# Stages of the last batch placed in the last iteration, with two buffers for x2

## The chip, the cores and the metric

The kernel runs on one core of a Trainium2 chip. The metric is the device time of one execution in microseconds (us). In the profile PE is TensorE (matrix multiply, PEld its weight loads), DVE is VectorE, ACT is ScalarE, POOL is GpSimd, SP is SyncE, which here issues every DMA.

## The reference, cut to what matters

```python
def reference(x, W_attn, W_proj, W, b, V_r, C):      # x: (4, 2048, 256)
    x = x + 0.5 * ffn(layernorm(x))                  # ffn(z) = z @ W.T + b + (z @ V_r) @ C.T
    x = x + attn(layernorm(x))
    x = x + 0.5 * ffn(layernorm(x))
    return x

# attn: 16 heads of width 16, causal; scores s = q.k / 4
# weight of a pair = polymax(s) = (s*s + 1 if s > 0 else 1 - s/100) / 1000   (no softmax sum)
# y = weights @ v; result y @ W_proj
```

## The kernel before

The 4 x 2048 rows are cut into 16 chunks of 512 rows (`NCH`), four to a batch (`CPB`). Each chunk goes through three stages. A (tables `A_*`): layer norm, z1T, ffn, giving x1. B (`B_*`): layer norm, q, k, v and the state sums. C (`C_*`): when the chunk's y is complete for all 16 heads, `proj` (y @ W_proj plus x1, into `x2`), layer norm `ln3` into `z3`, transposes `z3T`, `out` (the second ffn added to `x2`), and the store.

Attention runs as 16 iterations (`ITERS`): one for each batch and each group of four heads. An iteration has 40 tiles, so 80 half tiles: one in each slot of a hand-written plan (`order()`). In a slot TensorE does a half tile's scores, in each second slot the values matmuls of the tile three tiles back (`LAG`), and then the pieces of stage jobs that the plan places there. The scores lie in two PSUM buffers; DVE and ACT raise them into `rp`, POOL and ACT square them, TensorE sums them into y. Window c of an iteration is query chunk c; its y is complete, and copied by ACT (L806), at slots 13, 29, 53 and 83 (83 is slot 3 of the next iteration, or of what follows the last).

A stage table says at which slots after its start a job begins on TensorE: `C_SHORT` has proj at 0 and 4, ln3 from 8, z3T at 20 and 21, out at 22 and 26; `C_FULL` has 24 and 28, 32, 65 and 67, 71 and 75. A proj or out job has four pieces (slots) of 8 matmuls; two jobs make 64 matmuls. DVE empties a proj or out job one slot before the end of its four plus one (L889, L894), ACT empties z3T (L780). ln3 steps: DVE's statistics in steps 0 to 3, aggregation in step 4, scales in step 7 (L869 to L871), ACT's square root in step 8, POOL's normalisation in steps 8 to 11 (L686), the bias in steps 12 to 15 (L694). Each engine runs its instructions in the order of the slots.

SP's queue is ordered by slots too. `load_c` (L534, L535) loads `y_c` and `x1c` for a chunk, 12 slots ahead of proj at most. It waits until the chunk's y has been stored (`store_y`, L541) and until proj of the chunk before is emptied (there is one `y_c` and one `x1c`). The finished x2 is stored at L624; the first DVE write of the next chunk's proj waits for that store (`out_stored`), as there is one `x2`.

The plan before: C of chunk n-4 in iteration n from 4 to 14 (`C_FULL`). In iteration 15: chunk 11 at slot 0, chunk 12 at 27, chunk 13 at 54, all `C_SHORT`. After the last iteration (`drain`): five slots, then chunk 14 whole at slot 85 and chunk 15 whole at slot 117, counted from the start of iteration 15. What follows at `o.again` runs only if scores below -100 can occur; here it doesn't.

Of the kernel before, what the change touches and what calls it, by code (L numbers as in the profile page):

```python
# [12 lines left out]
P = 128  # L13
# [98 lines left out]
B_EARLY = {"qT": (0, 2), "k": (4, 8), "v": (22, 26), "kT": (30, 32), "state": (31, 33, 34, 35)}  # L112
C_SHORT = {"proj": (0, 4), "ln3": 8, "z3T": (20, 21), "out": (22, 26)}
# [80 lines left out]
def order():  # L194
# [10 lines left out]
    for n in range(1, ITERS):  # L205
        at = o.stretch(NHALF, range(NHALF))
        if n + CPB < NCH:
            o.stage(n + CPB, at, B_FULL)
        if n + CPB + 1 < NCH:
            o.stage(n + CPB + 1, at, A_FULL)  # L210
        if CPB <= n < ITERS - 1:
            o.stage(n - CPB, at, C_FULL)
    o.stage(NCH - 5, at, C_SHORT)
    o.stage(NCH - 4, at + 27, C_SHORT)
    o.stage(NCH - 3, at + 54, C_SHORT)
    assert o.next_half == ITERS * NHALF
    o.drain = o.n
    o.stretch(LAG + 2)
    o.stage(NCH - 2, o.stretch(32), C_SHORT)
    o.stage(NCH - 1, o.stretch(40), C_SHORT)  # L220
# [52 lines left out]
def build(nc, x_in, w_attn, w_proj, ffn_w, ffn_b, ffn_v, ffn_c, out):  # L273
    ctx = ExitStack()
    with ctx:
# [53 lines left out]
        x2 = sb("x2", [P, NB, DM])  # L329
# [147 lines left out]
        def _(sp):  # L477
# [73 lines left out]
            for x in o.jobs:  # L551
                if (x.kind, x.i) == ("ffn", 1):
                    put(x.empty_at + 1, "x1", x.chunk)
                if (x.kind, x.i) == ("qT", 1):
                    put(x.empty_at + 1, "qT", x.chunk)
                if (x.kind, x.i) == ("v", 1):
                    put(x.empty_at + 1, "v", x.chunk)
                if (x.kind, x.i) == ("state", NB - 1):
                    put(x.empty_at + 3, "state", x.chunk)
                if (x.kind, x.i) == ("kT", KC - 1):  # L560
                    put(x.empty_at + (2 if x.chunk < EARLY else 8), "parts", x.chunk)
                    if x.chunk < CPB:
                        put(x.empty_at + 5, "kq", 0, x.chunk)
                if (x.kind, x.i) == ("proj", 0):
                    put(max(x.start - 12, o.again if x.chunk >= NCH else 0), "c", x.chunk)
                if (x.kind, x.i) == ("out", 1):
                    put(x.empty_at + 1, "out", x.chunk)
            for n in range(ITERS):
                for c in range(CPB):
                    put(o.copy_slot[n * CPB + c] + 1, "y", n, c)  # L570
# [4 lines left out]
            def slot(s):  # L575
                for what, *args in at.get(s, ()):
# [43 lines left out]
                    if what == "out":  # L620
# [3 lines left out]
                        sp.dma_start(out_d[CH * c:CH * c + CH, :].rearrange("(i p) d -> p i d", p=P), x2[:]).then_inc(out_stored, 16)  # L624
# [22 lines left out]
        def _(pool):  # L647
# [30 lines left out]
            def normalise(k, src, dst, chunk, i):  # L678
                if i == 0:
# [4 lines left out]
                    if k == "ln2":  # L684
                        pool.wait_ge(job_done, o.made("z1T", chunk, 1))
                ins = pool.tensor_scalar(dst[:, i, :], src[:, i, :], rstd[k][:, i:i + 1], shift[k][:, i:i + 1],  # L686
# [17 lines left out]
            def slot(s):  # L704
# [20 lines left out]
                for k, chunk, step in o.steps.get(s, ()):  # L725
                    src, dst = {"ln1": (x_sb, z), "ln2": (x1, z), "ln3": (x2, z3)}[k]
# [129 lines left out]
        def _(dve):  # L856
# [10 lines left out]
            def scales(k, chunk):  # L867
                dve.wait_ge(sd_done[k], chunk + 1)
                nc.vector.reciprocal(rstd[k][:], sd[k][:]).then_inc(rstd_done[k], 1)  # L869
# [3 lines left out]
            def empty(x):  # L873
# [10 lines left out]
                if kind == "proj":  # L884
                    if i == 0:
                        dve.wait_ge(c_loaded, (a + 1) * 32)
                        if a > 0:
                            dve.wait_ge(out_stored, a * 16)
                    nc.vector.scalar_tensor_tensor(x2[:, 2 * i:2 * i + 2, :], two, 1.0 / DIVISOR, x1c[:, 2 * i:2 * i + 2, :],  # L889
                                                   ALU.mult, ALU.add).then_inc(done, 1)  # L890
                if kind == "out":
                    if i == 0:
                        dve.wait_ge(x2b_ready, a + 1)
                    nc.vector.tensor_tensor(x2[:, 2 * i:2 * i + 2, :], two, x2[:, 2 * i:2 * i + 2, :], ALU.add).then_inc(done, 1)  # L894
# [5 lines left out]
            def slot(s):  # L900
# [28 lines left out]
                for k, chunk, step in o.steps.get(s, ()):  # L929
                    x = {"ln1": x_sb, "ln2": x1, "ln3": x2}[k]  # L930
# [227 lines left out]
```

## Time and profile before

| | us |
|---|---|
| median of three runs | 1956.75 |
| lowest, highest | 1953.23, 1956.96 |
| the profiled execution, its own time | 1957.39 |
| its span, first to last instruction | 1955.6 |
| TensorE busy | 1667.1 (85%) |
| DVE, ACT, POOL busy | 1328.0, 1363.4, 1323.8 |
| mean granted TensorE clock | 0.964 |

Busy time is the sum of an engine's instructions. A stretch is read by cutting the span at a recurring instruction; here at ACT's copies of y (L806), of which there are 64, four to an iteration. "Idle before, releaser" tells how long an engine stood still before an instruction and which instruction ended that.

### The profile page before, as it was taken

How to read it: one execution, taken by the hardware profiler on the slowest of the kernel's cores; microseconds unless marked ns; L12 is line 12 of the kernel's file. 1: busy time of each engine (PE TensorE's matmuls, PEld its weight loads, DVE VectorE, ACT ScalarE, POOL GpSimd, SP SyncE). 2: the span in 40 equal slices, each digit the busy share in tenths (PEclk: the TensorE clock that was granted, in tenths of full speed). 3: DMA queues.
4: the chain of work that ended last, by engine and by line, in shares of the span. 5: the costliest groups of instructions: out<-in, count | busy, mean ns of one | idle time of the engine just before them, and what ended most of it. 6: DMA issues, size and time to landing. Idle time of an engine off the chain costs nothing.

```text
span 1955.6 us, 66923 instructions
## 1 busy us (share of the span) xinstructions
PE 1667.1 (85%) x27158; PEld 807.2 (41%) x27158; DVE 1328.0 (68%) x3313; ACT 1363.4 (70%) x2178; POOL 1323.8 (68%) x1419
## 2 busy tenths in 40 slices
PE   4687889898989899898989989898988889898884
PEld 2344334343434444353444435343444444434332
DVE  1465677776767777677777767777677777777652
ACT  1244568787878777777778778776877888886650
POOL 3354558787878767778776768877677767676552
PEclk9898889999999999999999999999999999999996
DMA  2343433332315242343424333341513231413111
GB/s 74 122 135 120 128 102 93 93 104 79 112 50 152 67 118 76 113 117 90 121 59 129 92 101 102 95 133 32 159 50 118 70 95 49 117 39 106 37 36 58
DMA packets 155190, 183.14 MB, mean 94 GB/s; under 512 B 22012, under 2 KB 129660, under 8 KB 152836
## 3 DMA queue, kind: packets, MB, share of 16 engines
q1 hardware_dynamic: 154884, 178.82, 31.3%
q8 instruction: 221, 3.62, 0.8%
q14 instruction: 85, 0.70, 0.1%
HBM read 102.43 MB, written 76.30 MB: 91 GB/s over the span
## 4 chain that ended last, share of the span: by engine, by line
PE 52%; ACT 17%; DVE 15%; issue 8%; POOL 4%; DMA 3%; SPq 0%; ACTq 0%; DVEq 0%; POOLq 0%
PE y_ps L977 19%; PE score L977 16%; PE bank L977 13%; DVE rp L912 9%; ACT rp L820 7%; ACT rp L836 4%; PE bank L1003 3%; ACT rp L840 3%; POOL z L686 2%; DVE lin L918 1%; DMA part_scratch<-parts 1%; ACT lin L826 1%; DVE qk_max L924 1%; DMA out_dram<-x 1%; DVE bnst_ln L937 1%
## 5 line engine op out<-in xcount | busy, mean ns | idle before, releaser
L912 DVE TENSOR_SCALAR rp<-score 128x512 f32<-128x512 f32 (+2 forms) x1728 | 944.2, 574 | 223.4 <-PE score L977 219.7
L977 PE MATMUL score<-qs,ks 96*32 96x512 bf16 (+3 forms) x10240 | 742.8, 354 | 169.5 <-DVE rp L912 86.1
L724 POOL TENSOR_TENSOR rp<-rp 128x1024 f32<-128x1024 f32 (+1 forms) x416 | 755.7, 1828 | 148.5 <-DVE rp L912 137.2
L820 ACT ACTIVATE rp<-score 128x512 f32<-128x512 f32 (+1 forms) x832 | 458.5, 592 | 292.3 <-PE score L977 289.8
L977 PE MATMUL y_ps<-rp,vt 128*16 128x512 f32 (+3 forms) x5120 | 598.6, 539 | 22.1 <-ACT rp L840 14.2
L977 PEld LDWEIGHTS score<-qs,ks 96*32 96x32 bf16 x10240 | 291.6, 96 | 599.0 <-DVE rp L912 314.1
L836 ACT ACTIVATE rp<-rp,rise 128x1024 f32<-128x1024 f32 (+1 forms) x416 | 464.1, 1145 | 1.4 <-POOL rp L699 1.4
L699 POOL TENSOR_SCALAR_AFFINE_SELECT rp<-rp 128x256 f32<-128x256 f32 (+1 forms) x384 | 184.1, 481 | 312.6 <-ACT rp L820 158.4
L840 ACT ACTIVATE rp<-rp 128x1024 f32<-128x1024 f32 (+2 forms) x224 | 291.1, 1305 | 121.3 <-POOL rp L699 67.6
L918 DVE SCALAR_TENSOR_TENSOR lin<-score,slope_mask 128x128 f32<-128x128 f32 x768 | 215.1, 280 | 0.0
L977 PEld LDWEIGHTS y_ps<-rp,vt 128*16 128x16 f32 x5120 | 133.6, 97 | 102.4 <-ACT rp L840 25.5
L977 PE MATMUL bank<-w_ffn,zT 128*32 128x256 f32 x2048 | 164.1, 411 | 7.4 <-ACT zT L780 7.4
L977 PE MATMUL bank<-w_qkv,z2T 128*32 128x256 f32 x2048 | 150.9, 386 | 9.7 <-ACT parts L797 9.7
L1003 PE MATMUL bank<-ident,z 128*128 128x128 f32 x384 | 70.5, 320 | 50.4 <-POOL z L686 48.1
L686 POOL TENSOR_SCALAR z<-x,rstd_ln,shift_ln 128x256 f32<-128x256 f32 x128 | 72.1, 569 | 59.6 <-DVE shift_ln L871 58.4
L977 PEld LDWEIGHTS bank<-w_ffn,zT 128*32 128x32 f32 x2048 | 70.5, 118 | 84.8 <-issue 54.9
L977 PE MATMUL y_ps<-lin,vt 128*16 128x128 f32 x2048 | 104.4, 273 | 0.0
L977 PEld LDWEIGHTS y_ps<-lin,vt 128*16 128x16 f32 x2048 | 60.4, 96 | 79.7 <-issue 67.4
L977 PEld LDWEIGHTS bank<-w_qkv,z2T 128*32 128x32 f32 x2048 | 65.9, 111 | 61.2 <-issue 27.5
L869 DVE RECIPROCAL rstd_ln<-sd_ln 128x4 f32<-128x4 f32 x48 | 8.5, 177 | 117.5 <-ACT sd_ln L849 117.5
L1003 PEld LDWEIGHTS bank<-ident,z 128*128 128x128 f32 x384 | 48.2, 160 | 89.6 <-issue 78.0
L686 POOL TENSOR_SCALAR z<-x_sb,rstd_ln,shift_ln 128x256 f32<-128x256 f32 x64 | 35.0, 556 | 69.2 <-DVE shift_ln L871 69.2
(78 smaller groups left out, 1392.9 us busy)
## 6 DMA issues: line engine op xcount, KB each, us to landing
part_scratch<-parts SPq DMA_DIRECT2D x16, 1536.0 KB, 7.5
qs<-part_scratch SPq DMA_DIRECT2D x384, 64.0 KB
ks<-part_scratch SPq DMA_DIRECT2D x384, 64.0 KB, 2.4
state_scratch<-st_new SPq DMA_DIRECT2D x16, 528.0 KB
st<-state_scratch SPq DMA_DIRECT2D x64, 132.0 KB
x_sb<-in_L_attn_x_dram SPq DMA_DIRECT2D x16, 512.0 KB, 4.3
x_scratch<-x SPq DMA_DIRECT2D x16, 512.0 KB, 5.3
qT_scratch<-qkT SPq DMA_DIRECT2D x16, 512.0 KB, 3.9
```

The costliest lines, as they stand in the source:

```text
L686: ins = pool.tensor_scalar(dst[:, i, :], src[:, i, :], rstd[k][:, i:i + 1], shift[k][:, i:i + 1], ALU.mult, ALU.add)
L699: pool.affine_select(out=block, in_=block, compare_op=ALU.is_ge, fill=fill, base=0, pattern=[[0, heads_in_it], [1, P]], channel_multiplier ...
L724: pool.tensor_tensor(half, half, half, ALU.mult).then_inc(squared["pool"], 1)
L820: nc.scalar.activation(rp[T % RP_BUFS][:, 2 + v, off:CH], score[H % S_BUFS][:, v, off:CH], ACT.Relu).then_inc(raised["act"], 1)
L826: nc.scalar.activation(lin[D % L_BUFS][:, 2 + v, :], score[H % S_BUFS][:, v, off:off + P], ACT.Copy, scale=SLOPE, bias=ONE).then_inc(lin_d ...
L836: nc.scalar.activation(part, part, ACT.Square, bias=rise[:]).then_inc(squared["act"], 1)
L840: nc.scalar.activation(whole, whole, ACT.Square).then_inc(squared["act"], 1)
L912: nc.vector.tensor_scalar(rp[T % RP_BUFS][:, 2 * u + v, off:CH], score[H % S_BUFS][:, v, off:CH], 0.0, RISE, ALU.max, ALU.add).then_inc(ra ...
L918: nc.vector.scalar_tensor_tensor(lin[D % L_BUFS][:, 2 * u + v, :], score[H % S_BUFS][:, v, off:off + P], ONE / SLOPE, slope_mask[:, 0, :], ...
L924: nc.vector.tensor_reduce(qk_max[:, x.chunk, j:j + 1], qkT[:, j, :], AX.X, ALU.max, apply_absolute_value=True).then_inc(bounded, 1)
L977: return nc.tensor.matmul(*args, start=start, stop=stop, skip_group_check=True)
L1003: ins = nc.tensor.transpose(dst[:, P * blk:P * blk + P], src[:, blk, P * i:P * i + P], ident[:])
```

## The change

`x2` gets two buffers, used by turns of chunks. So the first DVE write of proj(a) waits for a-1 stores and not for a. The plan of stage C changes from iteration 12 on. Iteration 12 holds chunks 8 and 9 (new table `C_HALF`, 40 slots each), 13 and 14 hold chunks 10 and 11 (`C_FULL`). Iteration 15 holds chunk 12 at slot 20 and chunk 13 at slot 50 (`C_SHORT`), and chunk 14 at slot 60 (`C_LATE`, the same figures as `C_SHORT`): its proj is at slots 60 and 64, its z3T at 80 and 81, its out at 82 and 86. Chunk 15 starts at slot 92. A load of C is now issued no earlier than the slot after the chunk's y is copied, and the store of y goes to the head of its slot on SP. Two guards are added: POOL's normalisation ln3 waits until z3T of the chunk before is done, and DVE's scales wait until POOL has used those of the chunk before. By the slots of the plan the load of chunk 12 stands in slot 14, that of 13 in slot 38, that of 14 in slot 54 and that of 15 in slot 84.

```diff
@@ -110,6 +110,8 @@
 A_FIRST = {"z1T": (12, 13), "ffn": (14, 18), "z2T": (34, 35), "ln1": 0, "ln2": 22}
 A_EARLY = {"z1T": (12, 13), "ffn": (14, 18), "z2T": (38, 39), "ln1": 0, "ln2": 22}
 B_EARLY = {"qT": (0, 2), "k": (4, 8), "v": (22, 26), "kT": (30, 32), "state": (31, 33, 34, 35)}
+C_HALF = {"proj": (0, 6), "ln3": 10, "z3T": (24, 26), "out": (28, 34)}
+C_LATE = {"proj": (0, 4), "ln3": 8, "z3T": (20, 21), "out": (22, 26)}
 C_SHORT = {"proj": (0, 4), "ln3": 8, "z3T": (20, 21), "out": (22, 26)}
 
 AGGR, SCALES, ROOT, NORM, BIAS = NB, NB + 3, NB + 4, NB + 4, 2 * NB + 4
@@ -208,16 +210,22 @@
             o.stage(n + CPB, at, B_FULL)
         if n + CPB + 1 < NCH:
             o.stage(n + CPB + 1, at, A_FULL)
-        if CPB <= n < ITERS - 1:
+
+
+        if CPB <= n < ITERS - CPB:
             o.stage(n - CPB, at, C_FULL)
-    o.stage(NCH - 5, at, C_SHORT)
-    o.stage(NCH - 4, at + 27, C_SHORT)
-    o.stage(NCH - 3, at + 54, C_SHORT)
+        if n == ITERS - CPB:
+            o.stage(n - CPB, at, C_HALF)
+            o.stage(n - CPB + 1, at + NHALF // 2, C_HALF)
+        if ITERS - CPB < n < ITERS - 1:
+            o.stage(n - CPB + 1, at, C_FULL)
+    for c, s in ((NCH - 4, 20), (NCH - 3, 50)):
+        o.stage(c, at + s, C_SHORT)
     assert o.next_half == ITERS * NHALF
     o.drain = o.n
-    o.stretch(LAG + 2)
-    o.stage(NCH - 2, o.stretch(32), C_SHORT)
-    o.stage(NCH - 1, o.stretch(40), C_SHORT)
+    o.stage(NCH - 2, at + 60, C_LATE)
+    o.stretch(LAG + 9)
+    o.stage(NCH - 1, o.stretch(32), C_SHORT)
     o.again = o.n
     for c in range(NCH, 2 * NCH):
         o.stage(c, o.stretch(40), C_SHORT)
@@ -326,7 +334,7 @@
         y_sb = [sb(f"y_sb{i}", [P, CH]) for i in range(2)]
         y_c = sb("y_c", [P, KC, CH])
         x1c = sb("x1c", [P, NB, DM])
-        x2 = sb("x2", [P, NB, DM])
+        x2 = [sb(f"x2_{i}", [P, NB, DM]) for i in range(2)]
         z3 = sb("z3", [P, NB, DM])
         z3T = zT
 
@@ -562,12 +570,13 @@
                     if x.chunk < CPB:
                         put(x.empty_at + 5, "kq", 0, x.chunk)
                 if (x.kind, x.i) == ("proj", 0):
-                    put(max(x.start - 12, o.again if x.chunk >= NCH else 0), "c", x.chunk)
+                    last_y = o.copy_slot[(x.chunk // CPB * QUADS + QUADS - 1) * CPB + x.chunk % CPB] if x.chunk < NCH else o.again
+                    put(max(x.start - 12, last_y + 1), "c", x.chunk)
                 if (x.kind, x.i) == ("out", 1):
                     put(x.empty_at + 1, "out", x.chunk)
             for n in range(ITERS):
                 for c in range(CPB):
-                    put(o.copy_slot[n * CPB + c] + 1, "y", n, c)
+                    at.setdefault(o.copy_slot[n * CPB + c] + 1, []).insert(0, ("y", n, c))
                     if n + 1 < ITERS:
                         put(o.half_slot[2 * (n * NT + LAST[c]) + 1] + 2, "q", n + 1, c)
                         put(o.values_slot[n * NT + KEY_LAST[c]] + 1, "k", n + 1, c)
@@ -621,7 +630,7 @@
                         seq, = args
                         c = seq % NCH
                         wait_emptied(sp, "out", seq, 1)
-                        sp.dma_start(out_d[CH * c:CH * c + CH, :].rearrange("(i p) d -> p i d", p=P), x2[:]).then_inc(out_stored, 16)
+                        sp.dma_start(out_d[CH * c:CH * c + CH, :].rearrange("(i p) d -> p i d", p=P), x2[seq % 2][:]).then_inc(out_stored, 16)
 
             for s in range(o.again):
                 slot(s)
@@ -683,6 +692,8 @@
                         pool.wait_ge(job_done, o.made("z2T", chunk - 1, 1))
                     if k == "ln2":
                         pool.wait_ge(job_done, o.made("z1T", chunk, 1))
+                    if k == "ln3" and chunk > 0:
+                        pool.wait_ge(job_done, o.made("z3T", chunk - 1, 1))
                 ins = pool.tensor_scalar(dst[:, i, :], src[:, i, :], rstd[k][:, i:i + 1], shift[k][:, i:i + 1],
                                          ALU.mult, ALU.add)
                 if i == NB - 1:
@@ -723,7 +734,7 @@
                         half = buf[:, 0:2, off:CH]
                         pool.tensor_tensor(half, half, half, ALU.mult).then_inc(squared["pool"], 1)
                 for k, chunk, step in o.steps.get(s, ()):
-                    src, dst = {"ln1": (x_sb, z), "ln2": (x1, z), "ln3": (x2, z3)}[k]
+                    src, dst = {"ln1": (x_sb, z), "ln2": (x1, z), "ln3": (x2[chunk % 2], z3)}[k]
                     if 0 <= step - NORM < NB:
                         normalise(k, src, dst, chunk, step - NORM)
                     if 0 <= step - BIAS < NB and k != "ln2":
@@ -866,6 +877,9 @@
 
             def scales(k, chunk):
                 dve.wait_ge(sd_done[k], chunk + 1)
+                if chunk > 0:
+
+                    dve.wait_ge(z_ready[k], chunk)
                 nc.vector.reciprocal(rstd[k][:], sd[k][:]).then_inc(rstd_done[k], 1)
                 dve.wait_ge(rstd_done[k], chunk + 1)
                 nc.vector.scalar_tensor_tensor(shift[k][:], mv[k][:, :, 0], -1.0, rstd[k][:], ALU.mult, ALU.mult).then_inc(norm_ready[k], 1)
@@ -884,14 +898,14 @@
                 if kind == "proj":
                     if i == 0:
                         dve.wait_ge(c_loaded, (a + 1) * 32)
-                        if a > 0:
-                            dve.wait_ge(out_stored, a * 16)
-                    nc.vector.scalar_tensor_tensor(x2[:, 2 * i:2 * i + 2, :], two, 1.0 / DIVISOR, x1c[:, 2 * i:2 * i + 2, :],
+                        if a > 1:
+                            dve.wait_ge(out_stored, (a - 1) * 16)
+                    nc.vector.scalar_tensor_tensor(x2[a % 2][:, 2 * i:2 * i + 2, :], two, 1.0 / DIVISOR, x1c[:, 2 * i:2 * i + 2, :],
                                                    ALU.mult, ALU.add).then_inc(done, 1)
                 if kind == "out":
                     if i == 0:
                         dve.wait_ge(x2b_ready, a + 1)
-                    nc.vector.tensor_tensor(x2[:, 2 * i:2 * i + 2, :], two, x2[:, 2 * i:2 * i + 2, :], ALU.add).then_inc(done, 1)
+                    nc.vector.tensor_tensor(x2[a % 2][:, 2 * i:2 * i + 2, :], two, x2[a % 2][:, 2 * i:2 * i + 2, :], ALU.add).then_inc(done, 1)
                 if kind == "state":
                     if a * NB + i >= 2:
                         dve.wait_ge(st_added, a * NB + i - 1)
@@ -927,7 +941,7 @@
                     if b < EARLY:
                         split(dve, b, i, step)
                 for k, chunk, step in o.steps.get(s, ()):
-                    x = {"ln1": x_sb, "ln2": x1, "ln3": x2}[k]
+                    x = {"ln1": x_sb, "ln2": x1, "ln3": x2[chunk % 2]}[k]
                     if step == 0:
                         if k == "ln1":
                             dve.wait_ge(x_loaded, (chunk + 1) * 16)
```

## Rows read from the trace of the kernel before

**Rows 1.** The page, part 1: busy time and share of each engine.

```profile
PE 1667.1 (85%) x27158; PEld 807.2 (41%) x27158; DVE 1328.0 (68%) x3313; ACT 1363.4 (70%) x2178; POOL 1323.8 (68%) x1419
```

**Rows 2.** Windows cut at last copies: span, length, PE, PEld, DVE, ACT, POOL, PEclk.

```profile
508.37:611.54 103.17, 92.07 (x1564) 44.07 (x1560) 75.50 (x191) 83.58 (x135) 79.83 (x83) 1.00 0.32 94
611.54:724.12 112.58, 101.09 (x1700) 49.40 (x1696) 80.58 (x204) 85.09 (x138) 84.45 (x91) 0.98 0.34 101
...
1505.75:1598.04 92.29, 81.93 (x1356) 38.02 (x1352) 69.64 (x171) 75.11 (x117) 65.88 (x67) 1.00 0.28 76
...
1690.93:1784.03 93.10, 84.27 (x1396) 39.20 (x1392) 69.43 (x169) 75.11 (x117) 65.94 (x67) 0.98 0.32 87
1784.03:1905.18 121.15, 99.44 (x1492) 44.51 (x1484) 76.95 (x184) 74.02 (x113) 71.80 (x75) 0.94 0.16 47
1905.18:1955.60 50.42, 24.23 (x290) 14.20 (x282) 11.66 (x36) 3.39 (x7) 9.87 (x16) 0.70 0.18 56
```

**Rows 3.** Chain's shares, then waits (total, times, longest us), in iteration 15.

```profile
by line: DVE rp L912 18.7%; PE y_ps L977 15.5%; PE bank L977 12.4%; PE score L977 10.8%; issue 9.1%; DMA out_dram<-x 5.0%; ACT rp L820 4.0%; ACT rp L840 3.2%; POOL rp L724 3.1%; PE bank L1003 2.7%; POOL z L686 2.7%; DVE bnst_ln L937 2.3%; D
...
DVE x L889 <- DMA out_dram<-x: 5.1, 2, 3.2
```

**Rows 4.** Timeline, ACT: copy of the first y of iteration 13 and of iteration 15.

```profile
1606.85 0.63 ACT L806 ACTIVATE y_sb<-y_ps 128x512 f32<-128x512 f32 x1
...
1794.84 0.63 ACT L806 ACTIVATE y_sb<-y_ps 128x512 f32<-128x512 f32 x1
```

**Rows 5.** DMA issues with median us to landing; timeline of two loads.

```profile
y_c<-y_scratch SPq DMA_DIRECT2D x16, 512.0 KB, 5.3
x1c<-x_scratch SPq DMA_DIRECT2D x16, 512.0 KB, 5.8
...
DMA to landing us min/median/max: 5.0/5.8/8.0
...
1799.64 0.40 SPq L534 DMA_DIRECT2D y_c<-y_scratch  x1
1800.09 0.47 SPq L535 DMA_DIRECT2D x1c<-x_scratch  x1
...
1875.77 0.69 DVE L889 SCALAR_TENSOR_TENSOR x<-bank,x1c 128x512 f32<-128x512 f32 x1 [3.15 <-PE bank L977]
1876.55 0.40 SPq L534 DMA_DIRECT2D y_c<-y_scratch  x1
```

**Rows 6.** Timeline, TensorE in iteration 13, slots 20 and 57 to 60.

```profile
1612.32 0.41 PE L977 MATMUL y_ps<-lin,vt 128*16 128x128 f32 x8
...
1655.52 0.83 PE L977 MATMUL score<-qs,ks 96*32 96x512 bf16 x12 [0.20 <-ACT lin L826]
...
1658.61 1.05 PE L977 MATMUL y_ps<-rp,vt 128*16 128x512 f32 x8 [0.23 <-POOL rp L724]
1659.46 0.41 PE L977 MATMUL y_ps<-lin,vt 128*16 128x128 f32 x8
```

**Rows 7.** Timeline, TensorE in iteration 15, z3T of chunk 11 and behind it.

```profile
1805.07 0.63 PE L1003 MATMUL bank<-ident,z 128*128 128x128 f32 x4 [1.60 <-POOL z L686]
...
1807.26 1.92 PE L977 MATMUL y_ps<-rp,vt 128*16 128x512 f32 x8
```

**Rows 8.** Timeline of the tail, after the last y.

```profile
1905.18 0.60 ACT L806 ACTIVATE y_sb<-y_ps 128x512 f32<-128x512 f32 x1 [0.94 <-PE y_ps L977]
...
1912.71 0.40 SPq L534 DMA_DIRECT2D y_c<-y_scratch  x1
...
1917.74 1.94 PE L1003 MATMUL bank<-ident,z 128*128 128x128 f32 x8 [8.31 <-POOL z L686]
...
1920.46 6.29 PE L977 MATMUL bank<-w_ffn,zT 128*32 128x256 f32 x64 [0.78 <-ACT zT L780]
...
1926.57 3.64 PE L977 MATMUL bank<-w_out,y_c 128*32 128x256 f32 x64
...
1932.47 1.29 DVE L889 SCALAR_TENSOR_TENSOR x<-bank,x1c 128x512 f32<-128x512 f32 x2 [4.96 <-DMA out_dram<-x]
```

## The prediction

> **What bounds the kernel now.** I read the page first [rows 1]: TensorE is busy 85% of the span, and the other engines about 70%. Then I cut the span at the copies of the last y of each iteration (slot 3 of the next one) and read each stretch [rows 2]. An iteration with stages A and B beside its attention takes 103.17 us, one with A, B and C 112.58, so one more C costs 9.41 us where TensorE is already full. An iteration with C alone takes 92.29 to 93.10 us, so attention alone takes some 83.2. The last iteration holds three C stages and takes 121.15 us: two more C at 9.4 would make 111.5, so some 10 us are lost to waits there. After the copy of the last y stand 50.4 us in which no engine is full: a serial tail. The change works on these two stretches and loads iteration 12 for it.
>
> Which wait ends last in the last iteration: DVE's proj emptying waits for the store of the chunk before, since both use x2. That is 5.1 us of DVE idleness, and this store holds 5.0% of the stretch on the chain of waits, 6.0 us [rows 3]. The rest are waits at z3T, whose normalisation on POOL stands just ahead of it [rows 7].
>
> **The edits, step by step.** Slots are those of the plan; I count them from the start of the iteration.
>
> **1. Iteration 12 gets C of chunk 9.** One C is 64 proj matmuls, 8 transposes, 64 out matmuls, plus two loads, one store, and the work of DVE, ACT and POOL. Its price as a whole is 9.4 us [rows 2]. C_HALF puts 14 slots between the end of proj and z3T, with 3 slots between POOL's last normalise step and z3T (C_SHORT has 1), so I add only 0.5 us. Sum +9.9. Bounds: 8.3 (bare TensorE work at full speed: 3.64 for 64 matmuls, twice, and half of the 1.94 us of 8 transposes at half speed [rows 8]) and 14.1 (each of the two further C in iteration 15: (121.15 - 92.9)/2). Chunks 10 and 11 only move up one chunk in iterations 13 and 14, at the place where 9 and 10 stood: nothing. Chunk 11's first proj pieces leave the end of stretch 14: -0.5.
>
> **2. The last iteration has less C.** Before, it holds C of 11, 12, 13 up to the last y, but for the last out piece, some 24.4 us of TensorE work. After, it holds 12, 13, proj and z3T of 14 and one piece of out, 8.3 x 2 + 3.6 + 1.0 + 0.5 = 21.7. The difference, 2.7 us, at the rate 9.4/8.3, is -3.1 us.
>
> **3. Two x2.** proj(a) waits for the store of a-2 instead of a-1. That takes away the 6.0 us on the chain. Nothing takes this wait's place, as the store of two chunks earlier issues many slots before. -6.0; bounds -5.1 (the idleness of DVE alone) and -7.7 (a slow stretch of the clock gone with it, 1.7 us, step 6).
>
> **4. A new wait at proj of chunk 12.** It moves from slot 27 to 20; its y is copied at slot 13 and its load is issued at 14 on SP. In iteration 15 the copy starts at 1794.84 and y_c is issued at 1799.64, 4.80 later: the four stores of y and their landing lie between. x1c goes 0.45 behind and needs 5.8 [rows 4, 5]. It lands at copy + 11.05. When does TensorE reach proj? In iteration 13, which has no work beside attention there, the copy of chunk 0 starts at 1606.85, and the last matmuls of slot 20 start at 1612.32 and are issued by 1612.54: copy + 5.7 [rows 4, 6]. So TensorE stands 11.05 - 5.7 = 5.3 us. Behind that instruction are queued all scores, on which DVE and ACT live (two score buffers), so that nothing hides it. I take 4.9 (the landing between its least, 5.0, and its median); bounds 0 (other engines catch up) and 5.5.
>
> **5. A new wait at proj of chunk 14.** proj 14 stands at slot 60; the single y_c is free when proj 13 is emptied at slot 57. The rows of chunk 13 before give this: DVE's second proj starts at 1875.77 just as the matmuls are done, and y_c is issued at 1876.55, 0.8 later [rows 5]. With 0.45 and 5.8 the load lands some 7.1 us after proj 13. From slot 57 to the job of slot 60 iteration 13 takes from about 1655.95 (a third into the score row) to 1659.68, 3.7 us [rows 6]. TensorE stands 3.4 us; bounds 0 and 4.1. SP blocks behind this wait, but its next entry is only the store of chunk 13.
>
> **6. The clock.** After a wait of 1.60 us of TensorE for z, eight y matmuls take 1.92 us instead of 1.05 [rows 6, 7]: half speed, 1.2 instead of 2.4 GHz. The stretch of iteration 15 has a granted clock of 0.94 against 0.98 to 1.00 before [rows 2]. Each new wait should bring one such stretch; two of them at 1.0 us (bounds 0 and 1.7): +2.0.
>
> The Trainium skill, "TensorE: Matmul & The Clock Gate", section "HAM oscillation — how this bites in real kernels", tells that a matmul burst shorter than the load behind it meets a cold array each time, and pays again at each wait. It speaks against putting proj so near to its load. By it both waits cost the whole slow stretch; a sum that left the clock out would be 2.0 lower here and another 3.2 lower in the tail. The trace agrees: 1.92 against 1.05 us.
>
> **7. The guards of z3 and of rstd.** POOL waits for z3T of the chunk before, and DVE's scales for POOL's z: 15 and 45 waits. For all but chunk 14 they are met tens of slots earlier. For 14, DVE reaches the scales at slot 75, POOL's normalise of 13 ends at 69. I take 0; bounds 0 and +3 (POOL six slots late). DVE stands there anyway for ACT's square root.
>
> **8. The tail.** Before, the copy of the last y ends at 1905.78 and the span 49.8 us later. In between stand the whole of chunk 14, then chunk 15: its proj starts at 1926.57, though its y_c was issued at 1912.71 already, and DVE then waits 4.96 us for the store of 14; from the end of its proj emptying, 1932.47 + 1.29 = 1933.76, to the end it is 21.84 us [rows 8]. After, only out of 14 is left (3.6 us) and the load sets the start: stores of y and landing 4.6 (between the 4.2 of chunk 12 and the 6.9 of the last), x1c 0.45 + 5.3: TensorE starts proj 15 at copy end + 10.3. It has been idle for about 7 us then. Before, 8.31 us idle led to 64 out matmuls in 6.29 us instead of the 3.64 of proj, half speed; so proj takes 6.8 us (64 matmuls at the 0.106 us of that fill), and DVE's last emptying 0.9 more: + 18.0. With 21.84 it is 39.8 instead of 49.8: -10.0. Bounds: -13.2 (proj at full speed) and -8 (stores as slow as in the last row, 6.9).
>
> **Sum**: 9.9 - 0.5 - 3.1 - 6.0 + 4.9 + 3.4 + 2.0 + 0 - 10.0 = +0.6 us. On the profiled execution's 1957.39 that is 1958.0; the median of the runs is 1956.75, so the forecast for a median is **1957.4 us**: no change. What the tail gives, the extra C in iteration 12 and the two load waits take back.
>
> **Rivals.** First, **the waits cost little** (faster). TensorE is idle for some 10 us of each light iteration [rows 2]; if these gaps close behind the waits, since DVE, ACT and POOL have caught up, steps 4, 5 and 6 fall from 10.3 to about 2: 1949. For it: POOL and ACT run slots late in the last iteration. Against it: the two score buffers tie DVE to TensorE at each half, and a lost 5 us is lost to both. Second, **a C in a crowded iteration costs 14 us** (slower). This is z3T reached before POOL's z, as in the last iteration, where each further C costs 14.1 instead of 9.4. If C_HALF in iteration 12 and proj 13 and 14 side by side do that, it is +4.7 for one and about as much for the two together: 1957.4 + 7 = 1964. It decides from the point where TensorE reaches z3T before POOL's last normalise step, as it did by 1.60 us for chunk 11 [rows 7]. Third, **the plan does less than it says**: z3T of 14 delays the last y, or the load comes late (x1c took 8.0 us once [rows 5]), so that proj 15 starts at copy + 14. Then the tail gives 6 instead of 10: 1961, just at the border. Fourth, **the tail gives all**, proj 15 at full speed and a quick load: -13.2, 1954.
>
> **How the numbers follow.** Forecast 0.42, with its own range 1953.5 to 1961.3. Waits cheap 0.26 (all faster). Crowded 0.17 (slower). Late load 0.08 (half slower). Full tail 0.07 (a third faster, two thirds within). A change below 0.2%, 3.9 us, can't be told from none. Of the forecast's own chance a tenth falls out on either side, 0.04 each. Faster: 0.26 + 0.02 + 0.04 = 0.32. Slower: 0.17 + 0.04 + 0.04 = 0.25. Within: 0.43. The range from 1947 to 1966 leaves out the outer parts of the first two rivals.
>
> **What would show it.** Step 1: iteration 12 at 102 us instead of 92.3. Steps 2 to 6: the last iteration at 121 to 122, with two waits of TensorE for x1c or y_c of 3 to 5 us ahead of w_out matmuls, and no wait of DVE's proj line for the store. Step 7: no wait of DVE's reciprocal for POOL. Step 8: 39.8 us from the last copy's end to the span's end, with the first proj matmul 10.3 us behind the copy. It is wrong if the last iteration falls under 115 us (first rival) or iteration 12 comes to 106 (second).

## The result and the profile after

The changed kernel takes 1947.5 us (median of four runs, 1944.8 to 1948.7) against 1956.9 before: ratio 0.9950, 95% interval 0.9936 to 0.9965. Measured once more beside its variants it was 1944.3 against 1954.6, ratio 0.9953 (0.9940 to 0.9967). So it is 0.5% faster, by 9.4 and 10.3 us, where no change was forecast. The profiled execution took 1944.84 us, with a span of 1943.1.

The page after, part 1, and the windows cut at the last copies, as in [rows 1] and [rows 2] (length, PE, PEld, DVE, ACT, POOL, granted clock; iterations 12, 13, 14, 15 and the tail):

```profile
PE 1663.6 (86%) x27158; PEld 808.4 (42%) x27158; DVE 1327.9 (68%) x3313; ACT 1364.3 (70%) x2178; POOL 1326.4 (68%) x1419
```

```profile
1499.96:1601.70 101.74, 90.71 (x1480) 43.34 (x1472) 76.87 (x190) 76.89 (x119) 71.10 (x75) 0.97 0.28 74
1601.70:1695.39 93.69, 83.47 (x1360) 38.21 (x1356) 69.61 (x171) 75.16 (x116) 66.04 (x67) 0.98 0.29 75
1695.39:1787.37 91.98, 82.00 (x1366) 37.89 (x1361) 69.65 (x171) 75.18 (x117) 65.98 (x67) 1.00 0.29 77
1787.37:1905.02 117.65, 97.09 (x1464) 44.94 (x1453) 74.99 (x179) 74.33 (x113) 71.94 (x75) 0.93 0.16 48
1905.02:1943.10 38.08, 17.50 (x202) 9.97 (x202) 7.49 (x22) 1.99 (x5) 4.94 (x8) 0.74 0.21 61
```

Where the 12.5 us between the two spans went:

| stretch | before | after | difference | forecast |
|---|---|---|---|---|
| up to the end of iteration 0 | 300.67 | 294.43 | -6.2 | 0 |
| iterations 1 to 11 | 1205.08 | 1205.53 | +0.5 | 0 |
| iteration 12 | 92.29 | 101.74 | +9.5 | +9.9 |
| iterations 13 and 14 | 185.99 | 185.67 | -0.3 | -0.5 |
| iteration 15 | 121.15 | 117.65 | -3.5 | +1.2 |
| tail | 50.42 | 38.08 | -12.3 | -10.0 |

The first row is not the change's. The same stretch of both kernels, before and then after:

```profile
0.00:300.67 300.67, 221.40 (x3144) 113.07 (x3148) 166.85 (x419) 130.77 (x226) 134.28 (x177) 0.88 0.37 114
```

```profile
0.00:294.43 294.43, 215.28 (x3144) 112.31 (x3148) 166.91 (x419) 130.76 (x225) 134.63 (x177) 0.91 0.38 117
```

The work is the same, 3144 matmul records, but TensorE was granted 0.91 instead of 0.88 and was busy 6.1 us less. In the runs below this stretch ends between 294.9 and 301.1 us, with either plan. It scatters, so the experiments are read from the last iterations and the tail, and the medians beside them. These windows scatter too: each is read from one profiled execution, and two such executions of the changed kernel (this one and a0 below) differ by 1.4 us in the last iteration, 1.1 in the tail and 3.0 in iterations 13 and 14. A difference of that size between two runs is not shown by their windows alone.

The two waits that were forecast, in the timeline of the changed kernel (start, us, engine, line, idle before and releaser). First chunk 12, whose y was copied at 1796.18:

```profile
1799.81 0.40 SPq L542 DMA_DIRECT2D y_c<-y_scratch  x1
1800.26 0.85 SPq L543 DMA_DIRECT2D x1c<-x_scratch  x1
...
1801.66 0.41 PE L991 MATMUL y_ps<-lin,vt 128*16 128x128 f32 x8
1805.49 1.08 PE L991 MATMUL bank<-w_out,y_c 128*32 128x256 f32 x8 [3.41 <-DMA x1c<-x_scratch]
1806.32 1.11 PE L991 MATMUL score<-qs,ks 96*32 96x512 bf16 x8
...
1836.44 0.63 PE L1017 MATMUL bank<-ident,z 128*128 128x128 f32 x4 [2.78 <-POOL z L697]
...
1867.92 0.64 PE L991 MATMUL bank<-w_out,y_c 128*32 128x256 f32 x8 [1.99 <-DMA x1c<-x_scratch]
...
1902.19 0.63 PE L1017 MATMUL bank<-ident,z 128*128 128x128 f32 x4 [1.89 <-POOL z L697]
```

The fifth line is chunk 12's scores behind the wait at half speed (1.11 us for eight; 0.64 in e7 below). The sixth is chunk 12's transposes, which wait 2.78 us for POOL's normalised z. The seventh is chunk 14's proj, the last its transposes, which wait for POOL just ahead of the last y's values. The tail, which answers to [rows 8]:

```profile
1905.02 0.60 ACT L817 ACTIVATE y_sb<-y_ps 128x512 f32<-128x512 f32 x1
1905.17 3.66 PE L991 MATMUL bank<-w_ffn,zT 128*32 128x256 f32 x64 [0.22 <-ACT zT L791]
1905.64 1.73 SPq L549 DMA_DIRECT2D y_scratch<-y_sb  x4
...
1908.63 0.40 SPq L542 DMA_DIRECT2D y_c<-y_scratch  x1
...
1914.98 5.99 PE L991 MATMUL bank<-w_out,y_c 128*32 128x256 f32 x64 [6.15 <-DMA x1c<-x_scratch]
...
1921.03 0.69 DVE L903 SCALAR_TENSOR_TENSOR x<-bank,x1c 128x512 f32<-128x512 f32 x1 [1.67 <-PE bank L991]
...
1926.85 1.94 PE L1017 MATMUL bank<-ident,z 128*128 128x128 f32 x8 [5.88 <-POOL z L697]
...
1929.57 5.53 PE L991 MATMUL bank<-w_ffn,zT 128*32 128x256 f32 x64 [0.78 <-ACT zT L791]
```

### The profile page after: what moved, and what is told of

It reads as the page before. It is cut to its first block, busy times and chain, and to the rows that moved or that the text cites. A ratio compares the mean times of both kernels' runs of the same rounds, so it can differ in the third digit from the quotient of the medians.

```text
span 1943.1 us, 66983 instructions
## 1 busy us (share of the span) xinstructions
PE 1663.6 (86%) x27158; PEld 808.4 (42%) x27158; DVE 1327.9 (68%) x3313; ACT 1364.3 (70%) x2178; POOL 1326.4 (68%) x1419
## 3 DMA queue, kind: packets, MB, share of 16 engines
q8 instruction: 222, 3.64, 0.8%
## 4 chain that ended last, share of the span: by engine, by line
PE 54%; ACT 16%; DVE 15%; issue 8%; POOL 4%; DMA 3%; SPq 1%; ACTq 0%; DVEq 0%; POOLq 0%
PE y_ps L991 20%; PE score L991 17%; PE bank L991 14%; DVE rp L926 9%; ACT rp L831 6%; ACT rp L847 4%; PE bank L1017 3%; ACT rp L851 3%; POOL z L697 2%; DVE lin L932 1%; DMA x1c<-x_scratch 1%; ACT lin L837 1%; DMA part_scratch<-parts 1%; DVE qk_max L938 1%; DVE rest L463 1%
## 5 line engine op out<-in xcount | busy, mean ns | idle before, releaser
L991 PE MATMUL bank<-w_ffn,zT 128*32 128x256 f32 x2048 | 159.5, 400 | 5.4 <-ACT zT L791 5.4
L991 PE MATMUL bank<-w_out,y_c 128*32 128x256 f32 x1024 | 81.9, 397 | 12.1 <-DMA x1c<-x_scratch 12.1
```

Of the source, the lines that this page charges most:

```text
L991: return nc.tensor.matmul(*args, start=start, stop=stop, skip_group_check=True)
```

## The experiments

In all of them "last iteration" is the stretch from the copy of the last y of iteration 14 to that of iteration 15, and "tail" runs from there to the end of the span. The slots of chunks 12 and 14 stand as (20, 60) for the changed kernel. Ratios are to the kernel before, run beside the variant. `...` marks what is left out of an edit.

### The parts of the change

**e1: order of SP's queue and guards alone, on the kernel before.**

```diff
-                    put(o.copy_slot[n * CPB + c] + 1, "y", n, c)
+                    at.setdefault(o.copy_slot[n * CPB + c] + 1, []).insert(0, ("y", n, c))
...
+                    if k == "ln3" and chunk > 0:
+                        pool.wait_ge(job_done, o.made("z3T", chunk - 1, 1))
...
+                if chunk > 0:
+                    dve.wait_ge(z_ready[k], chunk)
```

> The kernel before with two small parts of the change alone: the stores of y at the head of their slot on SP, and the two guards (z3 on POOL, rstd on DVE). Theory: neither is on the path; time as before, 1956.9 within 2 us, and the 6 us by which the changed kernel's profile reached the end of iteration 0 earlier (294.4 against 300.7) are scatter of the start. Rival: the order of SP's queue shortens iteration 0; then its last copy comes at 294 to 295 here too and the time is 1951.

Measured: 1957.6 against 1954.1, ratio 1.0024 (1.0004 to 1.0043). Iteration 0 ends at 297.8, the last iteration takes 127.9 us, 6.7 more than before, all of it between the copies of chunks 1 and 2. Both theories missed this. The timeline shows it:

```profile
1818.31 2.74 SPq L541 DMA_DIRECT2D y_scratch<-y_sb  x4
1821.09 0.42 SPq L624 DMA_DIRECT2D out_dram<-x  x1
1824.22 0.69 DVE L893 SCALAR_TENSOR_TENSOR x<-bank,x1c 128x512 f32<-128x512 f32 x1 [7.57 <-DMA out_dram<-x]
```

Both the store of y and the store of chunk 11's x2 stand in slot 30. With y first, x2's store waits behind ACT's copy and four issues, and DVE, which waits for it with one x2, stands 7.57 us instead of 3.2 [rows 3]. In the changed kernel, with two x2, no such wait is left; the order with two x2 wasn't tested by itself. The guards were not tested without the order; no wait for them stands out in the waits of the last iterations.

**e2: two buffers for x2 alone.** A store semaphore for each buffer, the plan as before.

```diff
-        x2 = sb("x2", [P, NB, DM])
+        x2 = [sb(f"x2_{i}", [P, NB, DM]) for i in range(2)]
-        out_stored = sem("out_stored")
+        out_stored = [sem(f"out_stored{i}") for i in range(2)]
...
-                        if a > 0:
-                            dve.wait_ge(out_stored, a * 16)
+                        if a > 1:
+                            dve.wait_ge(out_stored[a % 2], a // 2 * 16)
```

> The kernel before, with two buffers for x2 (and a store semaphore for each) and the plan as it was. Theory: DVE's waits for the store go, 6.0 us in the last iteration (121.2 to 115.5) and about 5 in the tail (49.8 to 44.7): 1946, as much as the whole change gives. Rival: another wait stands right behind the store's; the last iteration stays at 119 to 121 and the tail alone gives: 1952.

Measured: 1940.6 against 1954.1, ratio 0.9936 (0.9915 to 0.9957). The last iteration and the tail, in the windows:

```profile
1783.70:1898.74 115.04, 95.79 (x1491) 43.73 (x1483) 76.80 (x184) 74.09 (x112) 71.96 (x75) 0.97 0.17 50
1898.74:1942.80 44.06, 23.08 (x290) 13.78 (x282) 11.86 (x36) 3.40 (x7) 9.89 (x16) 0.77 0.21 65
```

115.0 against 121.2 and 44.1 against 50.4: the store waits cost 6.1 and 6.4 us. This one part gives at least what the whole change gives (0.9936 against 0.9950; the intervals overlap). The new plan adds nothing to it: against e2 the changed kernel has 9.8 us more in iteration 12, 1 to 3 more in the last iteration and 6 to 7 less in the tail.

**e3: chunk 14 back behind the last y**, the rest as changed.

```diff
-    o.stage(NCH - 2, at + 60, C_LATE)
-    o.stretch(LAG + 9)
-    o.stage(NCH - 1, o.stretch(32), C_SHORT)
+    o.stretch(LAG + 2)
+    o.stage(NCH - 2, o.stretch(32), C_SHORT)
+    o.stage(NCH - 1, o.stretch(40), C_SHORT)
```

> The changed kernel, with chunk 14 put back whole behind the last y (its proj no longer in the last iteration), the rest as changed. Theory (each stage C in an iteration costs 9.4 us, in the tail its proj is hidden behind the load of chunk 15 only in part): last iteration 117.7 to 106.5, tail 37.5 to 45: 1943.5, so faster than the changed kernel. Rival: chunk 14's advance is what pays; last iteration at 112, tail 50: 1954.

Measured: 1940.7, ratio 0.9930 (0.9903 to 0.9956); last iteration 107.2, tail 44.2. The theory's numbers came (106.5 and 45). The advance of chunk 14 at slot 60 costs 9 to 10.5 us in the last iteration and gives 6 to 7 in the tail. That is not the price of a C there: at slot 62 (e11 below) it costs 0.7 us in the last iteration, 107.9 against 107.2, and gives 3.9 in the tail.

**e9: the plan of before without chunk 11 in the last iteration**: e3 with the semaphores of e2 and chunks 12 and 13 at slots 27 and 54.

> Two buffers for x2 (a store semaphore each), C of chunk 9 in iteration 12, chunks 12 and 13 in the last iteration at the slots of before (27 and 54), 14 and 15 whole behind the last y: the plan of before without chunk 11 in the last iteration. With two x2 and chunk 11 there it took 115.0. Theory (chunk 11 at slot 0 costs more than a C elsewhere, as its z3T waits and the clock falls): 102 to 103, so 12 to 13 us for one C against 9.4 in iteration 12. Rival (a C costs 9.4 there too): 105.6. Tail 43.5 in both; time 1936 or 1940.

Measured: 1939.1, ratio 0.9934 (0.9909 to 0.9959); last iteration 105.6, tail 44.0. The rival was right to 0.1 us: taking chunk 11 out gives 115.0 - 105.6 = 9.4 us, the price of [rows 2].

### The waits for loads, and the slots

| run | slots | waits for loads | last iteration | PE busy | tail | ratio (interval) |
|---|---|---|---|---|---|---|
| a0, the change again | 20, 60 | 3.54, 1.78 | 116.2 | 96.0 | 37.0 | 0.9953 (0.9940-0.9967) |
| e5 | 25, 60 | -, 2.35 | 116.1 | 96.6 | 36.5 | 0.9957 (0.9942-0.9972) |
| e6 | 17, 60 | 7.11, 1.8 | 125.9 | 98.7 | 36.6 | 1.0012 (0.9997-1.0027) |
| e10 | 20, 60, z3T at 82 | 3.56, 1.86 | 112.7 | 93.1 | 37.1 | 0.9950 (0.9927-0.9974) |
| e11 | 20, 62 | 3.93, 0.28 | 107.9 | 90.9 | 40.3 | 0.9935 (0.9915-0.9956) |
| e4 | 25, 62 | -, 0.80 | 107.1 | 91.6 | 38.5 | 0.9918 (0.9890-0.9946) |
| e7 | 20, 60, x1c first | 2.97, 1.40 | 110.8 | 91.5 | 37.6 | 0.9939 (0.9909-0.9969) |
| e12 | 24, 62 | -, 0.41 | 99.2 | 89.1 | 40.1 | 0.9886 (0.9852-0.9920) |
| e13 | 25, 62, x1c first | -, 0.29 | 104.4 | 88.8 | 37.3 | 0.9911 (0.9883-0.9938) |
| e8 | 24, 62, x1c first | -, - | 98.5 | 88.7 | 36.9 | 0.9851 (0.9834-0.9869) |

Each was a change of numbers in one or two lines, and in e7, e8 and e13 of the order of loads; here for e4:

```diff
-    for c, s in ((NCH - 4, 20), (NCH - 3, 50)):
+    for c, s in ((NCH - 4, 25), (NCH - 3, 50)):
-    o.stage(NCH - 2, at + 60, C_LATE)
+    o.stage(NCH - 2, at + 62, C_LATE)
```

"x1c first" is this, in `load_c` (the arguments of the loads are cut):

```diff
-                    sp.wait_ge(y_stored[last_window % 2], (last_window // 2 + 1) * (16 * QH))
                     sp.wait_ge(x1_stored, (c + 1) * 16)
                 if seq > 0:
                     wait_emptied(sp, "proj", seq - 1, 1)
-                sp.dma_start(y_c[:], ...)
                 sp.dma_start(x1c[:], ...)
+                if seq < NCH:
+                    sp.wait_ge(y_stored[last_window % 2], (last_window // 2 + 1) * (16 * QH))
+                sp.dma_start(y_c[:], ...)
```

> The changed kernel with proj of chunk 12 five slots later (25 instead of 20) and chunk 14's C two slots later (62 instead of 60), so that TensorE reaches them about when their loads have landed. Theory (a wait of TensorE for a load costs its whole length, 3.4 + 2.0 us, and a slow stretch of the clock behind it): last iteration 117.7 to 111, 1941. Rival (the other engines' catching up absorbs it): last iteration unchanged within 1.5 us, 1947.

e4 gave more than its theory: 9 to 10.5 us off, not 6.7. Which of the two shifts did it?

> The changed kernel once more, beside its variants. Iteration 12 at 101.7, last iteration at 117.5, tail at 37.5 us; two waits of TensorE for x1c. Only iteration 0 may differ: 294 to 301 us if the start scatters.

> The changed kernel with proj of chunk 12 at slot 25 instead of 20, chunk 14 as changed. Theory (each wait for a load costs about twice its length, by the emptied pipeline and the slow clock behind it): the wait of 3.4 us goes, the one of 2.0 stays; last iteration 117.6 to 111. Rival (the two waits together make it, the second by pushing chunk 14 against the last y): 114 to 116.

> The changed kernel with C of chunk 14 two slots later (62), chunk 12 at slot 20 as changed. With 12 at 25 this took the last iteration from 116.1 to 107.1. Theory (the two are additive): 9 off the changed kernel's 116.2 to 117.7, so 107 to 109, and the first wait costs little. Rival (each wait costs by itself, twice its length): 111 to 112.

The two shifts in a square (a0, e5, e11, e4): chunk 14's two slots give 8.3 and 8.9 us, chunk 12's five give 0.1 and 0.7, although a wait of 3.5 us goes with them. e5's theory failed; its rival's number came. It doesn't follow that chunk 12's wait is free: 20 is an even slot and 25 an odd one, and from 25 to 24 the last iteration falls by another 8.0 us (e4 to e12, below). The shift to 25 takes a wait away and brings another loss of about its price.

> The changed kernel with z3T and out of chunk 14 two slots later (82 and 84), so that its transposes stand behind the last y's values and not ahead of them; proj of 14 stays at slot 60 with its wait for the load. Theory (z3T ahead of the last values, waiting for POOL's z, is what costs at the end): the stretch from chunk 2's to chunk 3's copy falls from 46.6 to 48.4 us to 43, the last iteration to 112 to 113. Rival (the wait for the load of 14 is the cost): unchanged, 116 to 117.

e10 splits chunk 14's 8.3 us: the transposes behind the last values give 3.5 (116.2 to 112.7; the stretch from chunk 2's copy to chunk 3's is 43.1, as expected), and the proj two slots later, with 1.6 us less of waiting for the load, gives the other 4.9 (112.7 to 107.9). The 3.5 us don't show in the medians (0.9950 against 0.9953).

> The changed kernel with proj of chunk 12 at slot 17, three slots earlier. The wait for its load grows by three slots, 3.4 to about 6 us. Theory (length plus a fixed part): last iteration 117.6 to 120.2. Rival (cost is twice the length throughout): 122.8. Second rival (no cost): 117.6.

The wait grew by 3.57 us and the last iteration by 9.7: more than either price. The wait itself:

```profile
1810.35 1.08 PE L991 MATMUL bank<-w_out,y_c 128*32 128x256 f32 x8 [7.11 <-DMA x1c<-x_scratch]
```

TensorE's busy time grew by 2.7 us for the same work, slower matmuls. The remaining 3.4 us can't be put down to the wait, as 17 is an odd slot too. e6 has a wait of TensorE for zT that the changed kernel doesn't have, the one that e12 and e13 below are about:

```profile
1848.32 0.64 PE L991 MATMUL bank<-w_ffn,zT 128*32 128x256 f32 x8 [2.54 <-ACT zT L791]
```

By stretches between the copies of y, e6 has 5.0 us more than a0 from chunk 0 to 1, where the wait for the load stands, 3.4 more from 1 to 2, where chunk 12's z3T stands, and 1.4 more from 2 to 3. So the 9.7 us are the price of the longer wait and of the odd slot together.

> The changed kernel with the load of x1c issued ahead of the wait for the stores of y, so that y_c alone (4.9 us from issue to landing, against 5.9 and 0.45 later) decides when proj can start. Both waits of TensorE get 1.3 us shorter, as does the start of the tail. Theory (a wait costs twice its length): last iteration 116.9 to 112, tail 37.5 to 36.2. Rival (a wait costs its length): 114.3.

The waits fell by 0.57 and 0.38 us only, but the last iteration by 5.4, and 4.5 of these are TensorE's busy time at the same work. The medians show less and not clear of the scatter, 0.9939 (0.9909 to 0.9969) against 0.9953. Behind the wait the matmuls now run at full speed (compare 1.08 and 1.11 above):

```profile
1806.29 0.64 PE L992 MATMUL bank<-w_out,y_c 128*32 128x256 f32 x8 [2.97 <-DMA y_c<-y_scratch]
1806.72 0.64 PE L992 MATMUL score<-qs,ks 96*32 96x512 bf16 x8
```

That the shorter wait did this isn't shown. In e3 the wait for chunk 12's load is as long as in a0, and yet the first eight matmuls behind it run at full speed and only later ones are slow:

```profile
1812.82 0.64 PE L991 MATMUL bank<-w_out,y_c 128*32 128x256 f32 x8 [3.56 <-DMA x1c<-x_scratch]
1813.25 0.81 PE L991 MATMUL score<-qs,ks 96*32 96x512 bf16 x8
1813.76 1.15 PE L991 MATMUL bank<-w_out,y_c 128*32 128x256 f32 x8
```

The tail didn't shrink as expected (37.6; a0 has 37.0): y_c is then what lands last.

> x1c first, chunk 12 at slot 24, chunk 14 at 62: the load waits out of the last iteration and the tail shorter. Theory: last iteration 107, tail 36.3 to 37, so 1935 to 1936, some 0.5% under the changed kernel. Rival (chunk 14's loads now wait at another place): 111, 1940.

e8 takes 1926.0 against 1951.9, ratio 0.9851: three times the change's gain. Its windows:

```profile
1789.53:1888.06 98.53, 88.69 (x1456) 43.69 (x1446) 72.31 (x179) 72.61 (x111) 68.91 (x71) 0.98 0.19 58
1888.06:1925.00 36.94, 17.57 (x210) 10.55 (x210) 7.48 (x22) 3.09 (x6) 7.73 (x13) 0.82 0.21 63
```

It differs from e4 in two things, the slot 24 for 25 and the order of the loads. e12 has only the first, e13 only the second:

> The combined version without its load order: chunk 12 at slot 24, chunk 14 at 62, y_c loaded first as in the changed kernel. Theory (the slot of chunk 12 is what took the last iteration from 107.1 at 25 to 98.5 at 24; the load order only shifts what is hidden by then): 100 to 102. Rival (the load order did it): 106 to 107.

> The combined version with chunk 12 at slot 25 instead of 24 (x1c first, chunk 14 at 62). Odd slots hold only a score half, even ones the values too, so that each piece and each transpose stands beside other work. Theory (the slot): last iteration back at 105 to 107. Rival (load order): 98.5 to 99.

It is the slot: 99.2 and 98.5 at 24, 104.4 and 107.1 at 25. The order of loads takes 3.2 us from the tail (40.1 in e12, 36.9 in e8). The intervals of the ratios overlap between e12 and either run at 25, so this rests on the windows, and on e15 below. e12 and e13 show a part of the cause. With chunk 12 at 25, z3T stands at slots 45 and 46 (e13):

```profile
1838.47 0.63 PE L1018 MATMUL bank<-ident,z 128*128 128x128 f32 x4 [1.75 <-POOL z L698]
...
1839.13 0.60 ACT L792 ACTIVATE zT<-bank 128x512 f32<-128x512 f32 x1 [1.88 <-PE bank L1018]
...
1839.63 1.90 ACT L852 ACTIVATE rp<-rp 128x2048 f32<-128x2048 f32 x1
...
1841.43 0.59 ACT L792 ACTIVATE zT<-bank 128x512 f32<-128x512 f32 x1
...
1842.16 0.64 PE L992 MATMUL bank<-w_ffn,zT 128*32 128x256 f32 x8 [1.38 <-ACT zT L792]
```

With chunk 12 at 24, at 44 and 45 (e12):

```profile
1831.46 0.63 PE L1017 MATMUL bank<-ident,z 128*128 128x128 f32 x4 [0.38 <-POOL z L697]
...
1832.50 0.59 ACT L791 ACTIVATE zT<-bank 128x512 f32<-128x512 f32 x1
...
1833.26 0.60 ACT L791 ACTIVATE zT<-bank 128x512 f32<-128x512 f32 x1 [0.17 <-PE bank L1017]
...
1833.80 1.91 ACT L851 ACTIVATE rp<-rp 128x2048 f32<-128x2048 f32 x1
...
1834.00 0.64 PE L991 MATMUL bank<-w_ffn,zT 128*32 128x256 f32 x8
```

ACT squares in odd slots. At an odd start the square of 1.9 us falls between the two emptyings of z3T, and TensorE stands in front of the out matmuls; at an even start both emptyings are ahead of it. The wait is 1.38 us of the 5 to 8 that the slot is worth. A second wait goes with it: the transposes themselves wait 1.75 us for POOL's z at slot 25 and 0.38 at 24 (2.78 at slot 20 of the changed kernel). The rest I haven't taken apart, so the squares are shown as one cause of the slot's price, not as the whole of it.

**e14** and **e15** carry the two findings to the plan of before with two x2.

> The kernel before with two buffers for x2 and x1c loaded first, and its plan unchanged. With two x2 alone: last iteration 115.0, tail 43.5. Its proj of 12 and 13 stand far behind their loads. Theory (the order of the loads pays only where a wait for them is left): unchanged, 1940. Rival (it pays by itself): last iteration under 110, 1934.

e14: 1943.6, ratio 0.9945 (0.9924 to 0.9965), with a last iteration of 118.2 us, no wait for a load in it, and a tail of 43.8. The order of the loads pays only where a wait for them is left; the 3.2 us more than in e2 have no cause that I could name (one slow stretch more: TensorE is busy 98.8 us instead of 95.8 for the same work).

```diff
-    o.stage(NCH - 4, at + 27, C_SHORT)
+    o.stage(NCH - 4, at + 28, C_SHORT)
```

> The kernel before with two buffers for x2 and chunk 12 at slot 28 instead of 27, nothing else. It tests the parity found with the changed plan on the plan of before. Theory (z3T at an even slot lets ACT empty both transposes ahead of its squares; at an odd one they lie on either side): TensorE's wait of 2.1 us for zT of chunk 12 goes, last iteration 115.0 (with two x2 alone) to 110. Rival (parity counts only in the changed plan's crowd): 114 to 116.

e15: 1933.3, ratio 0.9901 (0.9865 to 0.9938). One slot number took 6.1 us from e2's last iteration, and the times agree: all four of e15 (1930.1 to 1937.4) lie under all seven of e2 (1938.3 to 1946.9), with the kernel before at 1954.0 and 1954.1 beside them. Here the even slot is the later one and in e12 the earlier one, so it isn't the direction of the shift that pays. TensorE's wait for chunk 12's zT in e2, then the same and the window in e15:

```profile
1848.88 0.64 PE L979 MATMUL bank<-w_ffn,zT 128*32 128x256 f32 x8 [2.13 <-ACT zT L782]
```

```profile
1837.77 0.64 PE L979 MATMUL bank<-w_ffn,zT 128*32 128x256 f32 x8 [0.62 <-ACT zT L782]
```

```profile
1775.90:1884.86 108.96, 92.58 (x1492) 44.43 (x1484) 76.81 (x184) 73.99 (x113) 71.75 (x75) 1.00 0.18 53
```

## Why the prediction was wrong, point by point

**Step 1, C of chunk 9 in iteration 12**: +9.9 forecast, +9.5 measured. A price taken from two iterations that differ by just that stage [rows 2] held to half a us, and again for chunk 11 (9.4, e9 against e2). It doesn't hold for every place: see step 2.

**Step 3, two x2**: -6.0 forecast for the last iteration, -6.1 measured alone (e2). The chain of waits gave the price, DVE's own idleness (5.1) was a little low. What I didn't see is that this step alone makes the tail 6.4 us shorter.

**Steps 4 to 6, the new waits**: their places were right, their lengths too long (3.4 and 2.0 us, not 4.9 and 3.4). For chunk 12, SP issued y_c 3.6 us behind the copy's start instead of 4.8. For chunk 14, TensorE came 4.6 us behind the start of DVE's last emptying of proj 13 instead of 3.7. Their price was too low. Of the three things I had priced at 10.3 us together, chunk 14's wait is worth 4.9 (e10 to e11, for 1.6 us less of waiting) and chunk 12's 8.7 at most (e11 to e12, the whole of 20 to 24, with whatever else that shift changes; 2.4 us less of waiting for POOL's z is in it). So the first rival, that the waits cost little, is refuted. The slow clock, which I had put at 1.0 for each, has an uneven share: TensorE's busy time fell by 4.5 of the 5.4 us in e7, by 2.3 of the 4.9 from e10 to e11, and by 1.8 of the 8.7 from e11 to e12.

The Trainium skill's page "TensorE: Matmul & The Clock Gate", section "HAM oscillation — how this bites in real kernels", says that matmuls behind such a wait start on a cold array. The traces agree in part: 1.11 us for eight behind a wait of 3.41, but 0.64 for the first eight behind one of 3.56 (e3) and behind one of 2.97 (e7).

**Step 2, less C in the last iteration**: this is the step that failed most. I priced it by TensorE's work, -3.1 us. But with next to no waiting for loads (0.41 us) the last iteration comes to 99.2 us (e12) from 121.2, which is 22 less, and steps 2 and 3 together had 9.1 of that. Two terms make up most of the missing 12.9 us.

One is the slots, which I had priced at nothing. Before, chunk 12 stood at the odd slot 27 and TensorE waited 2.13 us for ACT's emptying of zT; the change moved it to an even one. e15 puts this at 6.1 us on the plan of before. The wait stood in the trace of before, and I had passed over it as "the rest", which I took for waits at z3T. The row of the timeline, and that of the waits (total, times, longest):

```profile
1850.02 0.64 PE L977 MATMUL bank<-w_ffn,zT 128*32 128x256 f32 x8 [2.13 <-ACT zT L780]
```

```profile
PE bank L977 <- ACT zT L780: 3.5, 2, 2.1
```

The other is the rate. I exchanged chunk 11 for chunk 14's proj and transposes by the work of TensorE. Chunk 11 gave its full 9.4 us (e9), but chunk 14's proj and transposes at slot 62 cost 0.7 us (e3 to e11) and not the 5 to 6 that this rate asks. TensorE's busy time grew by 1.5 us only: the last stretch was granted a clock of 1.00 in e11 and 0.96 in e3. So the exchange is worth 8.7 and not 3.1. With the slot's 6.1 and the 6.1 of the buffer that makes 20.9 of the 22 us; the rest is open. As all these are differences of single executions, the split is good to 2 or 3 us.

So for the last iteration two errors of opposite sign were added: the plan saves far more than I gave it, and the waits and the late transposes take back some 17 us instead of 10. The sum, +1.2, was off by 4.7 (117.65) to 6.1 (116.2).

**The second rival**, 14 us for a C in a crowded iteration, is refuted for iteration 12 by its 101.74 us. In the last iteration z3T does stand ahead of POOL's z, for chunks 12, 13 and 14 by 2.78, 1.45 and 1.89 us.

**The third rival** was half right: z3T of chunk 14 does stand ahead of the last values and waits (1.89 us) there. It costs 3.5 us (e10), and I had left it out of the sum.

**Step 7, the guards**: nothing, as forecast. The order of SP's queue, which I had not priced at all, costs 6.7 us in the last iteration with one x2 (e1); with two the wait that it lengthens is gone.

**Step 8, the tail**: -10.0 forecast, -12.3 measured. y_c was issued 3.0 us behind the copy's end (forecast 4.6), proj started at 9.4 (10.3) and took 5.99 us (6.8) as the clock rose within it (granted 0.50 from 1915 to 1919 and 0.81 from 1919 to 1921); the chain behind was 21.4 (21.84). The half speed itself came as forecast: at the 3.64 us of full speed proj would have taken 2.4 us less. My 0.106 us for a matmul isn't the rate of the row that I named: 6.29 us for 64 are 0.098, which gives 6.3 us.

**In sum**: forecast +0.6, measured -9.4 in the medians. The last iteration has 5 to 6 us of that error, the tail 2.3, iteration 12 0.4. The remaining 1 to 2 us lie within the scatter of the start, which moves single executions by up to 6 us. That the time fell just inside the range (1947.5, lower end 1947) was luck: the lower end was set by the first rival, whose mechanism is refuted, and the gain comes from terms that I had too small.

## What to carry to other kernels

Do the buffer before the plan: the second x2 alone gave at least as much (0.9936) as buffer and plan together (0.9950). The plan paid for an extra C in iteration 12 and put two matmul stages nearer to their loads than the loads take. A stage moved in a hand-written order must be checked against three rows: when its load lands, what its emptying engine does in the very slots of its transposes, and what stands behind it on the same queue. A short wait of TensorE cost more than its own length here: chunk 14's three times, for 1.6 us less of waiting (e10 to e11), chunk 12's some twice at most (8.7 for 3.9, e11 to e12). Moving the two stages by a few slots, with one order of loads, gave 1.0% more (e8). Compare slots of the same parity when a wait is to be priced; e5 and e6 mixed the two.

## What the runs showed of the hardware that I had not expected

The length of a wait alone doesn't tell the speed behind it. Behind 3.41 and 3.54 us the first eight matmuls took 1.08 us (the changed kernel, a0), behind 3.56 they took 0.64 (e3), behind 2.97 also 0.64 (e7), and behind 1.60 us the y matmuls ran at half speed, 1.92 us [rows 7]. What decides it isn't shown here.

The granted clock of the first 300 us differs from one execution to the next at the same instructions, 0.87 to 0.91, and the stretch takes 294.4 to 301.1 us. So two spans of this kernel can't be compared whole.
